# One D tile per image becomes an E tile: L1 attention with ScalarE's absolute values summed by TensorE for both images at once

## The reference, cut to what matters

```python
v = (x @ wqv_w.T + wqv_b).reshape(b, t, 3 * h, d)        # h = 8 heads, d = 64, t = 64 tokens
q, vf, vb = v[:, :, :h], v[:, :, h:2 * h], v[:, :, 2 * h:]
k = x[:, :, None, :] * wk[None, None]
a = -sum_w |q[b, s, h, w] - k[b, t, h, w]| / sqrt(64)    # scores [b, s, t, h]
a = concatenate([a, zeros(b, 1, t, h)], axis=1)
a = softmax(a, axis=1)[:, :t]
o = (einsum("bsdh,bshw->bdhw", a, vf) + einsum("bdsh,bshw->bdhw", a, vb)).sum(axis=2)
y = (o * sigmoid(1.702 * o)) @ fanin_w.T + fanin_b
return x + y
```

## Time and profile before

| | us |
|---|---|
| median of 3 runs | 2579.14 (2575.05 to 2579.5) |
| the profiled execution | 2576.05 |
| its span | 2574.2 |
| L1 attention in it, first to last difference | 720.5 to 2465 |
| granted TensorE clock, mean | 0.96 of full |

### The profile page before, as it was taken

How to read it: one execution, slowest core, us unless ns; L and a number is a source line. 1 busy time by engine, 2 the same in 40 slices (tenths; PEclk the granted TensorE clock), 3 DMA queues, 4 the chain that set the end, 5 groups by cost and what they waited for, 6 DMA issues and landing times.

```text
span 2574.2 us, 45353 instructions
## 1 busy us (share of the span) xinstructions
PE 2236.6 (87%) x12251; PEld 961.1 (37%) x12251; DVE 2244.8 (87%) x2638; ACT 1475.2 (57%) x3772; POOL 1767.2 (69%) x1033
## 2 busy tenths in 40 slices
PE   5558999999388989989989989899899899899878
PEld 3443333333123333333333333333333333333347
DVE  3877777777879999999999999999999999999974
ACT  0325555555146666666666666666666666666656
POOL 0112333333459889888888988888898888889843
PEclk8788999999689999999999999999999999999979
DMA  5200000000012112121211221221221212212201
GB/s 132 65 1 1 1 0 0 0 0 0 3 47 52 48 48 52 48 50 49 51 48 48 52 50 45 51 51 45 50 52 48 50 48 50 50 47 52 50 19 32
DMA packets 163216, 102.06 MB, mean 40 GB/s; under 512 B 55773, under 2 KB 161182, under 8 KB 163039
## 3 DMA queue, kind: packets, MB, share of 16 engines
q1 hardware_dynamic: 162858, 101.41, 16.0%
q10 hardware_dynamic: 316, 0.12, 0.0%
HBM read 10.63 MB, written 4.19 MB: 6 GB/s over the span
## 4 chain that ended last, share of the span: by engine, by line
PE 65%; DVE 23%; issue 9%; ACT 1%; DMA 1%; DVEq 0%; SPq 0%; POOL 0%; ACTq 0%; POOLq 0%
DVE score L1454 17%; PE pp L802 16%; PE pp L796 7%; PE pp L636 5%; PE pp L767 3%; PE pp L657 3%; PE pp L723 3%; PE pp L715 2%; PE pp L661 2%; PE pp L731 2%; PE pp L711 2%; PE pp L721 2%; PE pp L658 2%; PE pp L662 2%; PE pp L628 2%
## 5 line engine op out<-in xcount | busy, mean ns | idle before, releaser
L1454 DVE TENSOR_REDUCE score<-pp 128x16 f32<-128x1024 f32 x1408 | 1647.0, 1219 | 101.9 <-PE pp L802 82.2
L1571 POOL TENSOR_TENSOR absd<-absd 128x2560 f32<-128x2560 f32 x635 | 1442.4, 2271 | 197.1 <-ACT absd L1074 157.2
L802 PE MATMUL pp<-blocks,pick 128*128 128x512 f16 x2816 | 817.0, 383 | 155.0 <-DVE score L1454 150.4
L1074 ACT ACTIVATE absd<-pp 128x512 f32<-128x512 f32 x1280 | 695.4, 598 | 368.0 <-PE pp L796 364.1
L802 PEld LDWEIGHTS pp<-blocks,pick 128*128 128x128 f16 x2816 | 211.2, 98 | 590.7 <-DVE score L1454 421.9
L796 PE MATMUL pp<-blocks,pick 128*128 128x512 f16 x1280 | 400.0, 383 | 2.1
L1538 POOL TENSOR_TENSOR absd<-absd,yw 128x512 f32<-128x512 f32 x112 | 142.1, 1269 | 318.8 <-DVE yw L1376 318.8
L1008 ACT ACTIVATE absd<-pp 128x512 f32<-128x512 f32 x256 | 150.7, 596 | 148.1 <-PE pp L658 146.6
L1392 DVE SCALAR_TENSOR_TENSOR absd<-pp,absd 128x512 f32<-128x512 f32 x256 | 172.5, 688 | 52.9 <-ACT absd L1008 38.4
L796 PEld LDWEIGHTS pp<-blocks,pick 128*128 128x128 f16 x1280 | 119.8, 97 | 248.3 <-ACT absd L1074 84.6
L1056 ACT CAST qk<-pp 128x512 f16<-128x512 f32 x130 | 76.0, 585 | 191.2 <-PE pp L724 191.2
(11 more groups left out here) (227 smaller groups left out, 2497.9 us busy)
## 6 DMA issues: line engine op xcount, KB each, us to landing
blocks<-qk SPq DMA_DIRECT2D x1032, 64.0 KB, 2.0
attn<-score SPq DMA_DIRECT2D x1024, 16.0 KB, 1.8
xs<-xn SPq DMA_DIRECT2D x66, 32.0 KB, 1.8
big<-in_wrb_t SPq DMA_DIRECT2D x1, 2064.0 KB
big<-in_x_rows SPq DMA_DIRECT2D x4, 512.0 KB, 6.1
token_rows<-big SPq DMA_DIRECT2D x8, 256.0 KB, 2.0
big<-in_L_ffn_w SPq DMA_DIRECT2D x4, 512.0 KB, 10.1
out<-h SPq DMA_DIRECT2D x16, 128.0 KB, 2.0
```

The lines of the kernel that those rows point to most:

```text
L802: mm = pe.matmul(ps[bank + n], pick[:, unit % 8 + n, :], blocks[:, b, unit // 16, unit // 8 % 2, :], start=True, stop=True)
L1074: nc.scalar.activation(absd[odd][:, 16 * u + 8 * n:16 * u + 8 * n + 8, :], ps[4 + n].rearrange("p (h w) -> p h w", w=D), ACT.Abs).then_inc ...
L1454: dve.tensor_reduce(score[:, odd, b, 16 * d:16 * d + 16], pp[:, bank:bank + 2, :].rearrange("p n (h w) -> p (n h) w", w=D), AX.X, ALU.add, ...
L1571: nc.gpsimd.tensor_tensor(x[:, :, 0:w], x[:, :, 0:w], x[:, :, w:2 * w], ALU.add).then_inc(X["tree"], 1)
```

## The change

One D tile of each image becomes an E tile: `ORDER` is `DADDADDADDADADED`, with 10 D, 5 A and one E. For the E tile the operands of the matmul change places, so that what stands on the partitions is (head, element) and ScalarE writes the absolute values to a new part of `absd`. One pair later, TensorE sums both images' E tiles with a constant of ones (`sum_e`, 8 fp32 matmuls, four quarters of 32 partitions by two images, all into `ps[7]`), ScalarE copies the sums out (`copy_e`), TensorE turns them (`turn_e`, two small fp32 matmuls) and ScalarE puts them into `score` (`take_e`, semaphore `etaken`). `spread` waits for `etaken`. `low` no longer computes the projection again, but adds the negative high half to what still stands in bank 6. ScalarE normalises the weights, a head at a time in two parts, in place of GpSimd. The exponentials stand in four parts of two heads behind absolute(1, 2) to absolute(1, 5).

```diff
-ORDER = "DADDADDADDADDADD"
-ND, NA = ORDER.count("D"), ORDER.count("A")
+ORDER = "DADDADDADDADADED"
+ND, NP = ORDER.count("D"), ORDER.count("A")
+NA = NP + 1
...
             def spread(p, odd, b, first):
                 sp.wait_ge(X["red"], ND * (2 * p + b + 1))
                 sp.wait_ge(X["pooled"], 2 * p + b + 1)
+                sp.wait_ge(X["etaken"], p + 1)
...
             def low(p, odd, kind):
 
                 pe.wait_ge(X["half"], 4 * p + 2 * kind + 1)
-                if kind:
-                    pe.matmul(ps[6], xT1[:, odd, :], wk_diag[:].rearrange("p h d -> p (h d)"), start=True, stop=False)
-                else:
-                    pe.matmul(ps[6], xTq[:], wqv[:, 0:QK], start=True, stop=False)
-                pe.matmul(ps[6], neg_eye[:], qk[:, kind, 0, :], start=False, stop=True).then_inc(X["klo_ps" if kind else "qlo_ps"], 1)
+                pe.matmul(ps[6], neg_eye[:], qk[:, kind, 0, :], start=False, stop=True, skip_group_check=True).then_inc(X["klo_ps" if kind else "qlo_ps"], 1)
...
+            def sum_e(p, first):
+                pe.wait_ge(X["abs"], 4 * NA * (p + 1))
+                if not first:
+                    pe.wait_ge(X["etaken"], p)
+                for m in range(4):
+                    for b in range(2):
+                        mm = pe.matmul(ps[7][32 * m:32 * m + 32, 0:2 * P], pair_ones[:, b, :], abse[b][:, m, :],
+                                       start=(b == 0), stop=(b == 1))
+                mm.then_inc(X["e_ps"], 1)
+
+            def turn_e(p):
+                pe.wait_ge(X["esum"], p + 1)
+                for g in range(2):
+                    mm = pe.matmul(ps[7][:, 256 + 16 * g:272 + 16 * g], esum[:, P * g:P * g + P], row_of[:], start=True, stop=True)
+                mm.then_inc(X["et_ps"], 1)
...
+                        if k == 11 and at >= 1:
+                            sum_e(q - 1, at == 1)
+                        if k == 13 and at >= 1:
+                            turn_e(q - 1)
...
+            def copy_e(p):
+                act.wait_ge(X["e_ps"], p + 1)
+                act.wait_ge(X["et_ps"], p)
+                nc.scalar.copy(esum[:], ps[7][:, 0:2 * P]).then_inc(X["esum"], 1)
+
+            def take_e(p, odd, at):
+                act.wait_ge(X["et_ps"], p + 1)
+                if at >= 2:
+                    for b in range(2):
+                        act.wait_ge(X[f"spread{b}"], 16 * 8 * (p - 1))
+                nc.scalar.copy(score[:, odd, :, 240:256].rearrange("p b (g h) -> p g b h", g=2),
+                               ps[7][:, 256:288].rearrange("p (g b h) -> p g b h", g=2, b=2)).then_inc(X["etaken"], 1)
...
+            def normalise(p, part, first):
+                if part == 0:
+                    act.wait_ge(X["zr"], p + 1)
+                    if not first:
+                        act.wait_ge(X["o_ps"], p)
+                for n in range(4 * part, 4 * part + 4):
+                    op = nc.scalar.activation(attk[:, n, :], expd[:, n, 0:S], ACT.Copy, scale=zst[:, 1, n:n + 1])
                 if part:
-                    op.then_inc(X["exp"], 1)
+                    op.then_inc(X["attk"], 1)
...
-                absolute(s, 0, 3, first)
+                if at >= 2:
+                    normalise(q - 2, 0, at == 2)
+                absolute(s, 0, 3, q, first)
                 high_q(q + 1, False)
+                if at >= 1:
+                    copy_e(q - 1)
+                absolute(s, 0, 4, q, first)
                 low(q + 1, 0)
-                absolute(s, 0, 4, first)
+                if at >= 1:
+                    take_e(q - 1, 1 - odd, at - 1)
+                if at >= 2:
+                    normalise(q - 2, 1, at == 2)
+                absolute(s, 0, 5, q, first)
```

More of the change, by code:

```diff
@@ L97, in constants @@
         both[1, e, e // 2, e % 2] = 1.0 / LO_SCALE
+    row_of = np.zeros((4, 32, 2, 4, 2))
+    for m in range(4):
+        for b in range(2):
+            for a in range(2):
+                row_of[m, 2 * b + a, b, m, a] = 1.0
     same_head = np.kron(np.eye(16), np.ones((8, 8)))
@@ L147, in build @@
         absd0 = sb("absd0", [P, NA * 1024])
+        c_cols = absd0[0:7, 0:2048].rearrange("p (o c m) -> p o c m", o=2, c=8)
         kT = absd0[:, 2048:3072].rearrange("p (b a m) -> p b a m", b=2, a=4)
@@ L852, in _ @@
             fan_in(last - 2)
+            pe.wait_ge(X["sum"], last - 1)
+            sum_e(last, False)
+            turn_e(last)
+            pe.wait_ge(X["etaken"], PAIRS)
             def last_turn(p):
@@ L1066, in values_f, with absolute @@
                 nc.scalar.copy(vf[:, odd].rearrange("p i n d -> p (i n d)"), ps[6]).then_inc(X["vf"], 1)
-            def absolute(s, odd, u, first):
+            def absolute(s, odd, u, q, first):
                 for n in range(2):
@@ L1105, in pair @@
                 s, first = 2 * q, at == 0
-                absolute(s, 0, 0, first)
+                absolute(s, 0, 0, q, first)
                 if at >= 1:
@@ L1122, in pair @@
                 low(q + 1, 1)
-                absolute(s, 1, 0, first)
-                absolute(s, 1, 1, first)
+                absolute(s, 1, 0, q, first)
+                absolute(s, 1, 1, q, first)
                 if at >= 2:
                     turned_attn(q - 2)
-                absolute(s, 1, 2, first)
-                absolute(s, 1, 3, first)
+                absolute(s, 1, 2, q, first)
+                if at >= 1:
+                    exponentials(q - 1, 0, at == 1)
+                absolute(s, 1, 3, q, first)
                 if at >= 2:
@@ L1131, in pair @@
                 if at >= 1:
-                    exponentials(q - 1, 0, at == 1)
-                absolute(s, 1, 4, first)
+                    exponentials(q - 1, 1, at == 1)
+                absolute(s, 1, 4, q, first)
                 if at >= 1:
-                    exponentials(q - 1, 1, at == 1)
+                    exponentials(q - 1, 2, at == 1)
+                absolute(s, 1, 5, q, first)
+                if at >= 1:
+                    exponentials(q - 1, 3, at == 1)
             act.wait_ge(pads, PADS)
@@ L1151, in _ @@
             values_f(last, 1)
+            copy_e(last)
+            take_e(last, 1, 4)
             def root(c):
@@ L1171, in mlp_layer @@
                                          bias=wsel[g % 3][:, l, j, HID:HID + 1]).then_inc(M[f"h{l + 1}"], 1)
+            normalise(last - 1, 0, False)
+            normalise(last - 1, 1, False)
             turned_attn(last - 1)
@@ L1175, in _ @@
             turned_y(last - 1)
-            exponentials(last, 0, False)
-            exponentials(last, 1, False)
+            for part in range(4):
+                exponentials(last, part, False)
+            normalise(last, 0, False)
+            normalise(last, 1, False)
             root(0)
@@ L1206, in _ @@
                 dve.memset(t, 0.0).then_inc(pads, 1)
-            dve.wait_ge(pads, 14)
+            dve.wait_ge(pads, 15)
             for t in (xT4[D:D + 1, :], xT1[D:D + 1], xTq[D:D + 1, :], yT[D:D + 1, :], xT5[D:D + 1]):
                 dve.memset(t, 1.0).then_inc(pads, 1)
+            for half in range(2):
+                at = slice(64 * half, 64 * half + 64)
+                for b in range(2):
+                    dve.memset(pair_ones[at, b, 2 * b + half:2 * b + half + 1], 1.0)
             dve.memset(wk_bd[:], 0.0)
@@ L1574, in batch @@
                     pool.wait_ge(X[f"spread{b}"], 16 * 8 * (p - 1))
-                nc.gpsimd.tensor_tensor(score[:, odd, b, 16 * ND:256].unsqueeze(2), x[:, :, 0:1], x[:, :, 1:2],
+                nc.gpsimd.tensor_tensor(score[:, odd, b, 16 * ND:16 * ND + 16 * NP].unsqueeze(2), x[:, :, 0:1], x[:, :, 1:2],
                                         ALU.add).then_inc(X["pooled"], 1)
[L1578 to L1583, removed]
             def pair(q, odd, at):
```

72 lines of the change are left out of this document (47 added, 25 removed).

## The result

The changed kernel takes **2801.22 us** (median of 4 runs, 2800.54 to 2804.91) against 2579.14: a ratio of 1.0868, 95% interval 1.0849 to 1.0887. It is slower by 222 us, as forecast in kind; 2996 was predicted, and the range began at 2800.

What follows compares the result with a forecast made beforehand. VectorE sets the pace at 27.28 us a pair; the new loop through SyncE's queue takes 31.5, with low clock 33.8. 62 x 6.5 = 403 us plus about 14 behind the loop gives 2996 us, range 2800 to 3060.

Steps and rivals of the forecast that it cites:

- the loop's parts: From a pair's first D block: 7.31 to block 6, 2.18, sum_e 2.7, ScalarE 2.2, SyncE 17.1; sum 31.5 us.
- ScalarE's part: After sum_e: half an A block 0.44, two abs 1.1, cast of low queries 0.5, take_e 0.2; 2.2 us to etaken.
- three changes of quarter: TensorE's sum_e: 3.4 us serial less 0.7 saved in three changes of quarter, so 2.7 us; ends 0.9 and 3.4.
- L738's saving: TensorE's fp32 matmul with outputs in two halves: 8 records in 1.02 us, not 1.72; 0.70 saved in three changes.
- The rule of the Trainium skill: Matmuls with outputs in different groups of 32 partitions run concurrently; by that alone sum_e would cost 0.9 us.
- the clock: TensorE's clock falls to half at each pair's start; the first reduction comes 2.3 us later, loop 33.8 us.
- two D blocks, an A and an E after the first gap: TensorE's only work from about 27 to 31.5 us of a pair: 1.8 us of matmul, too little for full clock.
- quarters side by side: Rival: same loop at low clock, sum_e 0.9 in place of 2.7; 32.0 us a pair, 2884 us, 14%.
- a clock that mostly stays high: Rival: same loop, TensorE's clock stays high; 62 x 4.2 + 8 = 268 us more, 2847 us, 22%.
- Both signs of being wrong: A pair's first D block waits for a reduction, not a transfer; or the pair takes under 29 us.
- the case of a hidden wait: Rivals: wait hidden, TensorE's gaps decide; 27.6 us a pair, 2601 us, 5%; with sum_e at 0.9, 25.8, 2486 us, 3%.
- The tail: Behind the loop: last spread waits for sum_e and turn_e at low clock, pair 63 over 4 us longer; about 14 us.

Runs made afterwards that it cites:

- e7: Changed kernel with the first 128 score columns' transfers sent ahead of the etaken wait, and all eight sum_e matmuls writing the same 32 partitions: 2706.5 us, ratio 1.0496.
- e1: Kernel before with one wait added: spread(q-1) also waits until ScalarE has cast the low queries of pair q+1; 2795.56 us, ratio 1.0842.

## Why the prediction was right, and where its terms were off

**Right: the mechanism and its place.** spread waits for a sum that the same pair makes, the next pair's blocks are queued behind it, and the loop is longer than the pair was. The first D block waits for a transfer, the exponentials by their times for the scores, VectorE is at 76%. Shown from both sides: the wait alone makes the kernel before 8.4% slower, the change without it is 1.3% faster than the kernel before.

**Right: the loop's parts.** D block 6 at 7.30 (7.31 forecast), D block 7 at 2.26 more (2.18), ScalarE's part 2.10 (2.2), SyncE's 17.3 (17.1).

**Off: sum_e**, 2.7 us forecast, 1.03 measured. The step that failed is "sum_e, too, has three changes of quarter". I took L738's saving for one per change of half and carried it over. e7 gives the serial price, 3.58, and the four quarters divide it by 3.5: the times fit each quarter working through its own four records (0.86 us) while the others work through theirs, although in the list they stand one quarter behind the other. The rule of the Trainium skill, "TensorE: Matmul & The Clock Gate", Part 3, that stood beside the sum was the better guide: by it 0.9, and these runs agree with it, 1.03. With 1.03 the forecast loop is 31.5 - 1.7 = 29.8 us at full clock, and 30.0 was measured.

**Off: the clock**, 2.3 us in every pair forecast; measured about 1.6 in 27 of 63 pairs, 0.7 in the mean. The step that failed is that two D blocks, an A and an E after the first gap would in no pair keep it up. In 36 of 63 pairs the clock was at full level when the next pair began. The gap in front of the A block was 1.6 us, where I had worked out 2.5; the scores also went out 1.7 us earlier with the shorter sum_e. Where the gap in front of the pair was 2.7 us (e1), the clock was low at 62 of 64 starts. The 2.3 itself was too much as well: 1.5 by the two kernels with the wait alone. It came from the loop's start, where D block 1 still ran at the low clock. In the pair of 1543.41 D block 1 starts 3.60 us behind the pair's start (3.63 forecast), but the clock is back by then, and its reduction starts 0.71 later and not 1.14; that is 0.4 of the difference. The trace before had the price inside the loop, 28.9 against 27.2 us in the four pairs that began at half speed, and the prediction did not look there.

**Together**: two of my rivals held at once, quarters side by side and a clock that mostly stays high: 62 x (29.8 - 27.3) + 8 gives 2742 for full clock, 62 x 4.7 + 13 gave 2884 with it low everywhere, and the measured 2801 lies between them. I gave each alone a chance and their mixture none.

**Luck, and the signs that did not come.** That 2801 lies inside the range, 1 us above its lower end, is luck. The 2800 was set for a loop at full clock with a somewhat cheaper sum_e; with sum_e as measured that case is 2742, outside the range, and the low clock in 27 pairs brought the time back into it. The likeliest case, 2996, was 195 us too high. Of the signs named, the scores went out at 12.8 us (14 or more forecast), VectorE was at 76% (70%), the clock at 0.96 in the 1,400 us (under 0.95), and a pair took 30.7 us in the mean (31 to 34). Both signs of being wrong stayed away.

**Off: what the parts are worth without the wait.** The 1.7 us less of TensorE work (the low halves) and the 2.3 less of VectorE's stand in the prediction and add nothing to its sum. For the case of a hidden wait it counts 27.6 us a pair, or 25.8 with sum_e at 0.9; 26.7 was measured, between them. The low halves alone are worth 54 us, more than the 35 of the whole change without its wait.

**The tail**: 14 us forecast with the last pair, 10.2 measured behind the last values_b.

## What to carry to other kernels

A queue of transfers in program order has a load and a slack of its own that no share of busy time shows; before a wait is put into it, list what stands behind the waiting instruction and ask whether the thing waited for is made by the same round that the transfers behind it release. If so, the round is at least the sum of both ways, however idle each engine is. Put transfers that need no wait in front of it; and where two engines hand work over with two buffers, look for the gap between two handovers before adding up the engines' work.

## What the runs showed of the hardware that I had not expected

Sixteen fp32 records of 256 columns with outputs on 32 partitions took 1.03 us when they went to four quarters, four records to each in a row, and 3.58 us when all went to one. So, by these times, work for one quarter that is queued does not hold up the next quarter's.

TensorE's clock was low at the start of 27 of 63 pairs that are alike instruction for instruction. In each but the first few and the last there is a gap of 1.6 us in front of the last A tile and one in front of the next pair's first D block: 1.5 us, or 0.9 where the tiles between ran at half speed. The same gaps stand before starts at either level, as in these two pairs of the changed kernel that follow each other:

```profile
1575.20 0.60 PE L844 MATMUL pp<-blocks,pick 128*128 128x512 f16 x2 [1.53 <-DMA blocks<-qk]
...
1605.24 1.03 PE L844 MATMUL pp<-blocks,pick 128*128 128x512 f16 x2 [1.58 <-DMA blocks<-qk]
```

So neither the work nor the gaps tell which pair starts slow; all that the trace shows of an order is that no two slow starts follow each other. Idle matmuls in the gaps kept the clock at 1.00 over the 1,400 us, and the kernels with them are faster: 2755 against 2801 us, and 2704 against 2796 in the kernel with the wait alone.
